# A Macaron block on one core: attention's first group set among the last QKV tiles, and the dense projection set among its last two groups

## The reference

```
x = x + 0.5 * ffn(layernorm(x))      # W = base + mean|w-base| * sign(w-base) for w1, w3, w2
x = x + attention(layernorm(x))      # ffn: (silu(x W1) * (x W3)) W2, 1792 wide
x = x + 0.5 * ffn(layernorm(x))
```

## Time and profile before

| | us |
|---|---|
| median of 3 runs | 1591.8 |
| the profiled execution | 1592.39 |
| its span | 1590.7 |
| TensorE busy | 1474.8 (93%) |
| VectorE busy | 873.8 (55%) |
| ScalarE busy | 643.4 (40%) |
| GpSimd busy | 149.9 (9%) |
| mean granted TensorE clock | 0.973 |
| chain that ended last | PE 83%, DVE 9%, ACT 3%, issue 3% |

### The profile page before, as it was taken

How to read it: one execution, slowest core, us unless ns; L and a number is a source line. 1 busy time by engine, 2 the same in 40 slices (tenths; PEclk the granted TensorE clock), 3 DMA queues, 4 the chain that set the end, 5 groups by cost and what they waited for, 6 DMA issues and landing times.

```text
span 1590.7 us, 25041 instructions
## 1 busy us (share of the span) xinstructions
PE 1474.8 (93%) x9584; PEld 659.8 (41%) x9584; DVE 873.8 (55%) x1375; ACT 643.4 (40%) x903; POOL 149.9 (9%) x217
## 2 busy tenths in 40 slices
PE   0788999899999987799999999989999999999998
PEld 0233444344444443334343444324444444444443
DVE  7979432432544476899999999923431422412212
ACT  4464111121122254388888888781211112112111
POOL 0320000000000143012121212210000000000000
PEclk9989999999999998599999999999999999999999
DMA  9501800000000001000000000024000000000000
GB/s 389 195 0 53 354 0 0 1 0 0 1 0 1 1 1 34 1 2 2 2 2 3 2 3 2 2 102 177 0 0 0 28 0 0 27 0 1 27 0 27
DMA packets 16459, 57.38 MB, mean 36 GB/s; under 512 B 4848, under 2 KB 4848, under 8 KB 15856
## 3 DMA queue, kind: packets, MB, share of 16 engines
q1 hardware_dynamic: 16368, 56.11, 9.1%
HBM read 40.63 MB, written 15.20 MB: 35 GB/s over the span
## 4 chain that ended last, share of the span: by engine, by line
PE 83%; DVE 9%; ACT 3%; issue 3%; DMA 0%; POOL 0%; DVEq 0%; ACTq 0%; POOLq 0%
PE ps L1232 32%; PE ps L1253 16%; PE ps L1491 9%; PE ps L1406 7%; PE ps L1472 5%; PE ps L1393 3%; PE ps L1589 3%; PE ps L1279 2%; PE ps L1226 1%; DVE rowmax L1120 1%; PE ps L1501 1%; DVE wbase L877 1%; ACT probs L706 1%; PE ps L1365 1%; DVE w_raw L842 1%
## 5 line engine op out<-in xcount | busy, mean ns | idle before, releaser
L1232 PE MATMUL ps<-xt_hi,w_all 128*128 128x512 f16 x896 | 283.3, 388 | 42.3 <-DVE w_all L883 19.7
L706 ACT ACTIVATE probs<-ps 128x1024 f32<-128x1024 f32 (+3 forms) x384 | 294.1, 814 | 48.5 <-PE ps L1472 45.5
L1120 DVE TENSOR_REDUCE rowmax<-ps 128x2 f32<-128x1024 f32 (+3 forms) x208 | 237.1, 1140 | 15.7 <-PE ps L1414 7.4
L971 DVE SCALAR_TENSOR_TENSOR hb<-ps,scal,silub 128x512 f32<-128x512 f32 x56 | 42.0, 751 | 266.6 <-PE ps L1232 266.6
L1406 PE MATMUL ps<-ka,qa 48*128 48x512 f16 (+3 forms) x768 | 165.7, 345 | 15.4 <-DVE rowmax L1120 9.2
L1232 PE MATMUL ps<-xt_lo,w_all 128*128 128x512 f16 x448 | 173.9, 388 | 0.0
L1491 PE MATMUL ps<-probs,vs 128*32 128x512 f32 (+3 forms) x1536 | 164.4, 500 | 1.4 <-ACT ctx_sb L725 0.8
L1232 PEld LDWEIGHTS ps<-xt_hi,w_all 128*128 128x128 f16 (+1 forms) x896 | 89.4, 100 | 155.9 <-issue 46.0
L1124 DVE TENSOR_REDUCE rowmax<-ps 128x1 f32<-128x512 f32 x192 | 131.2, 684 | 16.3 <-PE ps L1406 13.5
L1472 PE MATMUL ps<-qa,ka 50*128 50x512 f16 (+3 forms) x768 | 133.3, 330 | 3.7 <-ACT probs L706 3.0
L1253 PE MATMUL ps<-w32b_all,hhib 128*128 (+1 forms) x448 | 133.3, 379 | 0.0
(11 more groups left out here) (154 smaller groups left out, 2160.8 us busy)
## 6 DMA issues: line engine op xcount, KB each, us to landing
spill<-w_all SPq DMA_DIRECT2D x1, 10752.0 KB, 28.8
w32b_all<-spill SPq DMA_DIRECT2D x1, 7168.0 KB, 20.9
x<-x_in SPq DMA_DIRECT2D x4, 1024.0 KB, 5.3
y_out<-x SPq DMA_DIRECT2D x4, 1024.0 KB, 4.2
wbase<-m1t SPq DMA_DIRECT2D x4, 896.0 KB, 12.7
w_raw<-w1t SPq DMA_DIRECT2D x4, 896.0 KB, 14.2
wbase<-m3t SPq DMA_DIRECT2D x4, 896.0 KB, 24.3
w_raw<-w3t SPq DMA_DIRECT2D x4, 896.0 KB, 24.3
```

The source lines that it names most:

```text
L706: nc.scalar.activation(probs[u % PBUF][:, 2 * pair:2 * pair + 2, 0:q1 - q0], wide(("scores", g, (u, pair)))[:, :, 0:q1 - q0], ACT.Exp, sca ...
L971: nc.vector.scalar_tensor_tensor(out=bufs["h"][u][:, :], in0=ps[:, UP, :], scalar=scal[:, 1:2], in1=bufs["silu"][u][:, :], op0=ALU.mult, o ...
L1120: nc.vector.tensor_reduce(dst, src, AX.X, ALU.max).then_inc(pair_taken, 1)
L1232: last = mm(ps[:, bank, :], w[a][:, k, bass.ts(t, P)], xt[b][:, k, :], start=(k == 0 and n == 0), stop=(k == HB - 1 and n == 2))
```

## The change

**Front.** The first 10 QKV tiles run as before. Then group 0's q and k are transposed, and each of tiles 10 to 15 is issued with four pieces of group 0 set into it: first half, two pieces, second half, two pieces. Group 1's three transposes follow tiles 13, 14 and 15. Piece 24 follows, and the loop starts at k = 1. The VectorE order is rewritten in the same way. On ScalarE, group 0's three `take_qk` stand ahead of tile 10, and group 1's behind the `high_parts` of tiles 12, 13 and 14.

**Dense.** `w_dense` is scaled and split into fp16 parts by GpSimd in the gaps of the masks in periods 4, 5 and 6; its bound is reduced by VectorE after period 1 and turned into a scale after period 2; four DMAs put the parts in place in period 7. GpSimd adds the dense bias to `x`, two tiles in each of periods 7 to 14. The projection is three fp16 passes. Its 8 tiles of batch 0 are set into the written-out order of periods 16 and 17; transposed rows and product use one bank (4 or 5 by the tile's parity). VectorE makes both parts of the transposed rows for tiles 0 to 7; for tiles 8 to 15 ScalarE makes the high one.

ScalarE, front:

```diff
-        for i in range(TOKEN_TILES):
+        for i in range(EARLY):
...
             take_raw(i)
...
+            take_v(i)
             if i:
                 high_parts(i - 1)
-        high_parts(TOKEN_TILES - 1)
         for o in range(3):
             take_qk(0, o)
+        for i in range(EARLY, TOKEN_TILES):
+            take_raw(i)
+            take_v(i)
+            high_parts(i - 1)
+            if i >= TOKEN_TILES - 3:
+                take_qk(1, i - TOKEN_TILES + 3)
+        high_parts(TOKEN_TILES - 1)
```

VectorE, front, and the two new calls behind periods 1 and 2 (`largest_dense` is one reduce of 128 x 2048 fp32 in SBUF, `dense_scale` is nine small chained instructions):

```diff
+        for i in range(EARLY, TOKEN_TILES):
+            r = 4 * (i - EARLY)
+            reduce_piece(0, r)
+            add_turned(i - 1)
+            reduce_piece(0, r + 1)
+            low_parts(i - 1)
+            reduce_piece(0, r + 2)
+            along(i)
+            reduce_piece(0, r + 3)
+        add_turned(TOKEN_TILES - 1)
+        reduce_piece(0, NP_ - 1)
+        split_rowmax(0)
+        low_parts(TOKEN_TILES - 1)
+        for k in range(1, GROUPS):
...
+            if k == 1:
+                largest_dense()
+            if k == 2:
+                dense_scale()
```

TensorE, front:

```diff
+        for i in range(EARLY, TOKEN_TILES):
+            r = 4 * (i - EARLY)
+            qkv(i, 0)
+            score_piece(0, r)
+            score_piece(0, r + 1)
+            qkv(i, 1)
+            score_piece(0, r + 2)
+            score_piece(0, r + 3)
+            if i >= TOKEN_TILES - 3:
+                transpose_qk(1, i - TOKEN_TILES + 3)
+        score_piece(0, NP_ - 1)
+        for k in range(1, GROUPS):
```

GpSimd, between `mask_unit(k - 2, 8)` and `mask_unit(k - 1, 0)` of the loop:

```diff
+            if k == 4:
+                for n in range(HB):
+                    dense_scaled(n)
+            if k == 5:
+                for n in range(HB):
+                    dense_high(n)
+            if k == 6:
+                for n in range(HB):
+                    dense_low(n)
+            if 7 <= k < 15:
+                bias_x(2 * (k - 7))
+                bias_x(2 * (k - 7) + 1)
```

TensorE, the projection and parts of the order of the tail:

```diff
+        def project(i, q):
...
+            for n, (a, b) in enumerate(PASSES):
+                last = mm(ps[:, rows_bank(i), :], ctx_t[i % 2][a][:, q, :], wd[b][:, q, :], start=(q == 0 and n == 0),
+                          stop=(q == HB - 1 and n == 2))
...
+        scores_t(14, 8, 0)
         transpose_rows(0)
+        scores_t(14, 8, 1)
+        project(0, 0)
+        values(14, 6)
...
+        project(4, 3)
+        scores_t(15, 8, 0)
+        project(5, 0)
+        scores_t(15, 8, 1)
+        project(5, 1)
+        values(15, 6)
+        scores_t(15, 9, 0)
+        transpose_rows(6)
+        project(5, 2)
+        scores_t(15, 9, 1)
+        project(5, 3)
+        values(15, 7)
+        scores_t(15, 10, 0)
+        project(6, 0)
...
+        for i in range(SEQ_TILES, TOKEN_TILES):
+            project(i, 0)
             if i + 1 < TOKEN_TILES:
                 transpose_rows(i + 1)
...
+            for q in range(1, HB):
+                project(i, q)
```

The VectorE order of the tail (excerpt):

```diff
+        context_high(5)
+        context_low(5)
+        normalise(15, 0)
+        add_dense(4)
+        norm_stats(8)
+        context_high(6)
+        context_low(6)
+        add_dense(5)
+        normalised(8)
...
+        for i in range(SEQ_TILES, TOKEN_TILES):
+            if i + 1 < TOKEN_TILES:
+                context_low(i + 1)
+            add_dense(i)
```

More of the change, by code:

```diff
@@ L103 @@
 ]
+EARLY = 10
+FIRST_TURNS = [("qk", 0, 0), ("qk", 0, 1), ("qk", 0, 2), ("qkv", 0, 10), ("qkv", 0, 11), ("qkv", 0, 12), ("qkv", 0, 13),
+               ("qk", 1, 0), ("qkv", 0, 14), ("qk", 1, 1), ("qkv", 0, 15), ("qk", 1, 2)]
 def turns(period, first):
     out = list(first)
-    for k in range(GROUPS + 2):
-        out += [(what, k - lag, n) for what, lag, n in period if 0 <= k - lag < GROUPS and (what, k - lag) != ("qk", 0)]
+    for k in range(1 if first else 0, GROUPS + 2):
+        out += [(what, k - lag, n) for what, lag, n in period if 0 <= k - lag < GROUPS]
     return {use: n for n, use in enumerate(out)}
 TURN = turns(SINGLE_TURNS, [])
-WIDE = turns(WIDE_TURNS, [("qk", 0, o) for o in range(3)])
+WIDE = turns(WIDE_TURNS, FIRST_TURNS)
 def unit_cols(u):
@@ new lines, in _ @@
+        values(14, 9)
+        scores_t(14, 11, 0)
+        project(1, 1)
+        scores_t(14, 11, 1)
+        transpose_rows(2)
+        values(14, 10)
+        scores_t(15, 0, 0)
+        project(1, 2)
+        scores_t(15, 0, 1)
+        project(1, 3)
+        values(14, 11)
+        scores_t(15, 1, 0)
+        project(2, 0)
+        transpose_context(14, 0)
+        scores_t(15, 1, 1)
+        project(2, 1)
+        values(15, 0)
+        scores_t(15, 2, 0)
+        transpose_rows(3)
+        scores_t(15, 2, 1)
@@ new lines, in _ @@
+        project(2, 2)
+        scores_t(15, 3, 0)
+        project(2, 3)
+        values(15, 1)
+        scores_t(15, 3, 1)
+        project(3, 0)
+        project(3, 1)
+        scores_t(15, 4, 0)
+        transpose_rows(4)
+        values(15, 2)
+        scores_t(15, 4, 1)
+        project(3, 2)
+        scores_t(15, 5, 0)
+        project(3, 3)
+        values(15, 3)
+        transpose_context(14, 1)
+        scores_t(15, 5, 1)
+        project(4, 0)
+        scores_t(15, 6, 0)
+        project(4, 1)
@@ new lines, in _ @@
+        scores_t(15, 10, 0)
+        project(6, 0)
+        values(15, 8)
+        scores_t(15, 10, 1)
+        project(6, 1)
+        values(15, 9)
+        scores_t(15, 11, 0)
+        transpose_rows(7)
+        scores_t(15, 11, 1)
+        project(6, 2)
+        values(15, 10)
+        values(15, 11)
+        project(6, 3)
+        project(7, 0)
+        transpose_context(15, 1)
+        project(7, 1)
+        transpose_rows(8)
+        project(7, 2)
+        project(7, 3)
+        for i in range(SEQ_TILES, TOKEN_TILES):
+            project(i, 0)
```

256 lines of the change are left out of this document (174 added, 82 removed).

## The result

| | us | ratio to before, 95% interval |
|---|---|---|
| kernel before, 6 runs | 1591.34 | 1 |
| changed kernel, 6 runs | 1602.98 (1597.45 to 1608.45) | 1.0073 [1.0056, 1.0090] |
| changed kernel again, 6 runs (`e_again`, below) | 1599.73 (1597.69 to 1606.84) | 1.0059 [1.0043, 1.0074] |

The change costs 8 to 12 us, where a gain of 10 was forecast. Its times lie in two groups: of the twelve, eight are 1597.5 to 1600.9 and four 1606.8 to 1608.5. The profiled execution is of the upper one, 1608.45, which is 16.1 above that of before.

The account below looks back on a forecast made before the run. TensorE and VectorE were taken as all but full in steady periods, so gains lay at front and tail: 1592.39 + 5.5 (front) + 3.5 (VectorE insertions) - 19.2 (tail) = 1582.2, less 0.6: 1581.5 us; range 1572 to 1590.

Parts of the forecast that it names:

- The front, +5.5: Interleaved QKV tiles 10 to 15: marker 0.5 us earlier at full clock, plus 6 for half clock; bounds 0 and 20.
- the prediction's own marker: End of the front: the first reduce of group 1, at 654.59 in the kernel before.
- half of six halves, 6: Interleaved tiles: half of six second halves caught at half clock (2.06 each, piece some 0.3), one doubled piece group more: 6 us.
- I give it nothing: First mixed period, 27.6 us against 25.6: no change, with 1 either way.
- The VectorE insertions, +3.5: Between periods 1 and 2, and 2 and 3: `largest_dense` 2.2, `dense_scale` 1.8, slack absorbing 0.5; bounds 0 and 4.
- TensorE waits for those after two pieces: Ends of periods 1 and 2: the next group's reduces queue behind the VectorE insertions, and TensorE waits for them.
- GpSimd in the gaps, 0: Gaps of 8.67 us ahead of a group's first mask: GpSimd's added work costs 0; bounds 0 and 4.
- they fit; cost 0 while the gap covers them: Mask gaps of 8.67 us: four subtractions make 6.0, two bias additions 3.0, so no cost.
- The tail, -19.2: Final attention and dense projection: sum 82.1 us, second FFN starting at 1123.5 instead of 1142.73; bounds -26 and -12.
- GpSimd late: Rival, mask gaps: operations at twice the row, subtractions pass the gap by 3.3, the rest by 1: 1586 us; 5%.
- Ring at half clock: Rival, interleaved tiles: every turn's second half caught at half clock, front +20 instead of +5.5: 1596 us; 7%.
- the front's bounds: Half-clock term of the interleaved front: 0 if never caught, 20 us if always.

Follow-up runs that it names:

- e_again: The changed kernel run once more with nothing altered: 1599.73 us, ratio 1.0059 to the kernel before.
- e_dense_only: The changed kernel with the old front (all 16 QKV tiles first, group 0 alone in period 0): 1592.98 us, ratio 1.0012 to the kernel before.
- e_lent_scale: The changed kernel without largest_dense, all-reduce and dense_scale; dense weights take the QKV weights' scale: 1583.94 us, ratio 0.9958 to the kernel before.
- e_pauses: The kernel before with four unused VectorE reductions (512, 1024, 2048, 2048 columns) behind groups 4, 7, 10, 13: 1602.44 us, ratio 1.0075.

## Why the prediction was wrong, step by step

- **The front, +5.5; measured +7.8 by the prediction's own marker (662.36, just past the 653 to 662 stated), and +1.0 in what is left of period 1.** In the ledger these are +7.0 and +1.8. The mechanism is shown: `high_parts(i-1)` behind `take_raw(i)` makes a ring, and one line takes it away. Evictions came every 10.7 us on average, within the forecast 9 to 12, and the clock was 0.80, within 0.7 to 0.9. The waits came as one or two per turn, at most 3.78. The term "half of six halves, 6" was too small: the turns sum to 53.5 against 45.8 at full clock. By its own prices, 2.06 and 0.3 for each caught half, three halves are 7.1 and not 6. "I give it nothing" for period 1 missed the 1.0, whose cause no run took apart.
- **The VectorE insertions, +3.5; measured +5.2 and +7.5.** The step that failed is "TensorE waits for those after two pieces", costed by length alone. The lengths were right (2.27 and 1.6 against 2.2 and 1.8), and so was the view that they are paid for nearly in full: at full clock the two come to 2.2 (`e_dense_only`) and 1.6. The text had costed half clock in the ring, from the earlier trace rows, and didn't ask here whether the wait that it had just found lets the clock fall too. Behind the first it did in each execution of the changed kernel that was profiled (+5.2, +6.7), behind the second in one of two. That one is the profiled execution of the upper group: at the clock of `e_again` the second insertion is +1.6, and the two together +8.3 against the 3.5 taken.
- **GpSimd in the gaps, 0; measured +6.1.** The step that failed is "they fit; cost 0 while the gap covers them". The additions, casts and subtractions did fit: steady periods stay at 25.5 to 25.6. What doesn't fit is what GpSimd needs to get ready behind an all-reduce, and its price was on the row that was read for its mean: "<-issue 6.9" in the earlier trace rows, once, ahead of a run of element-wise instructions. In the kernel before's timeline that run starts at 85.96 and is the first behind two all-reduces at 78.3 to 79.1. The diff adds an all-reduce in period 2, and the prediction didn't count it among the instructions added.
- **The tail, -19.2; measured -11.8.** The waits found in the new order are the right ones, 1.0 and 3.0 forecast, 1.44 and 2.24 measured. The step that failed is the same as for the insertions: each wait was costed by its length. Where the clock stays at 1.00 the same order gives -16.2 (`e_lent_scale`); the other 4.4 are half clock behind these two waits. Of the remaining 3.0, a tile of the second batch at 3.44 (1133.17 to 1136.61) against the 3.02 and 0.2 taken makes 1.8. With both waits all but gone the tail gives -19.4.
- **The rivals.** None was it. "GpSimd late" had the right engine, but by a wrong reason (slower instructions, 4.5 us) and in the wrong period: it had the subtractions of period 6 late by their length, and late were the multiplications of period 4, by the 7.39 ahead of them. "Ring at half clock" forecast a loss of this size in one place; the front lost 7 to 8 of the 20 that it gave, and the rest came in periods 2 to 4 and in the tail, each time as a wait of 1.4 to 4.3 with half clock behind it (in period 3 in one execution of two).
- **The range** ended at 1590. Only the front's bounds had half clock in them; the others took a wait by its length. In the profiled execution the ledger's excess over the forecast is 3.3 in front and period 1, 9.2 for the insertions, 6.1 for GpSimd and 7.4 in the tail: 26.0, all in the same direction. Against the lower group's times the forecast still misses by 16 to 19.

## What to carry to other kernels

In a stretch where two engines are full, ask of every small insertion not how long it is but which queue it stands in, what the next instruction of that queue releases, and whether the engine that then waits loses its clock: spread it over places where its engine already waits. Count the kind of instruction too: here an all-reduce on GpSimd was preceded by 5.8 us of standing still and the first `tensor_scalar` behind it by 7 more, and a dummy instruction in a gap paid the second in advance. `MODIFY_POOL_CONFIG` in its queue shows where. And where an overlap is built by hand, follow one tile around all engines: one eviction queued ahead of a copy cost 20 us here, and without it the overlap gives 11.7.

## What was not expected of the hardware

- Single TensorE waits of 1.4 to 2.2 us, far below the 4.28 of the earlier trace rows, are followed by half clock for 3 to 13 us in some executions and by none in others: 2.18 cost 2.2 and 5.3 in the same execution of `e_pauses`. What decides which was not found; the same wait, in the same program, fell on both sides. The Trainium skill (TensorE: Matmul & The Clock Gate, A second HAM failure mode) says that often repeated short idle spells between groups of matmuls can make the clock swing; here one wait amid full work did.
- So a program without any change has two times, some 8 us apart (twelve executions of the changed kernel; ten of `e_dense_only` show the same with the old front), while the kernel before stays within 2.7 us in 27.
- GpSimd stands still for 5.8 to 6.0 us ahead of an all-reduce and for 6.9 to 7.4 us ahead of the first element-wise instruction behind it, even 56 us later, while masks in between run at once: the first one starts 2.0 behind the start of its exponentials (705.57, 707.58), as in the kernel before (742.81, 744.82).
